# A fused cross-attention and mixture-of-experts kernel: slot numbers, products that read nothing and last sums moved, and the first chunk's queries projected in two halves

## The chip, the cores and the metric

The kernel runs on one core of a Trainium2 chip. A core has TensorE (PE, matmuls and transposes), VectorE (DVE), ScalarE (ACT), GpSimd (POOL) and SyncE (SP, which here only issues transfers). The metric is the device time of one execution in microseconds; lower is better. The kernel before was timed three times, and one more execution was profiled.

## The reference, cut to what matters

```python
x = x + tanh(g_xattn[0]) * xattn(layernorm(x), ctx)      # 32 sequences of 64 rows, 256 wide
# xattn: q, k_new, v_new = x @ wq.T, x @ wk.T, x @ wv.T
#        k, v = concat(cache, new);  softmax(q @ k.T / 16) @ v @ wo.T
x = x + tanh(g_ffn[0]) * ffn(layernorm(x))
# ffn: router = xf @ gate_w.T; softmax; top 2 of 8 experts
#      expert: (silu(xf @ fc1.T) * (xf @ fc2.T)) @ proj.T, 176 wide, weighted by the router
#      shared: the same with 704, times sigmoid(xf @ shared_gate_w.T)
```

All 2048 rows pass through both parts. The cache of keys and of values is the context, 64 rows for each sequence.

## The kernel before, in words

The program is written out by hand: for each engine there is one list of instructions, and semaphores tie the lists together. An engine takes its list strictly in order, so an instruction that waits holds up all that stand behind it on its engine.

A float32 operand is kept as two parts, "hi" (rounded to fp32r) and "lo" (the rest). A product is then a chain of three matmuls: hi*hi, hi*lo, lo*hi. For nearly every result in PSUM (the eight banks `B[0]` to `B[7]`) ACT copies it into a hi tile and DVE subtracts that from the bank into a lo tile; the next chain on PE waits for both. In the names of tiles `ew`, `sw`, `xt` and `sh` are large tiles that hold queries, keys, values, normalised rows and weights at different times.

The attention goes in four chunks `c` = 0 to 3 of 512 rows, each in four tiles `j` of 128 rows. While chunk `c` is attended, chunk `c+1` is normalised (`first_norm`, transposes on PE) and projected (`project`: `i` = 0, 1 the queries, 2, 3 the keys), and chunk `c-1` is normalised a second time and routed. For a tile: `scores` (PE), `row_max` (DVE), `exps` (ACT), `values` (PE), `v_hi` (ACT), `v_lo` (DVE), `probs_t` (PE), `probs_hi` (ACT), `probs_lo` (DVE), `attend` (PE), `residual` (DVE: reciprocal, scaled sum, statistics). `attend` waits in its second matmul for `v_lo` and in its third for `probs_lo`.

The router: `two_best(c)` and `counts(c)` on DVE find the two experts of each row and count them, `route(c)` on PE (two small matmuls) adds up the counts, `slots(c)` on DVE (seven small steps, each of which waits for the one before) makes of them a slot number for each row and expert, and `scatter(c, i)` on POOL writes the rows to these slots in DRAM with indirect transfers. The loops over `c` handle `slots(c-2)`, so slots of chunk 0 and 1 are made in loops 2 and 3.

Start: SP loads x of chunk 0 in two halves, then the four attention weights in three pieces, the context of chunk 0 (into `CR`), and x of chunk 1. ACT loads the gates, the constants (with the identity that transposes need) and the router's weights. `cached_hi(0)` (ACT) and `cached_lo(0)` (POOL, four subtractions) bring the context in as keys; behind `cached_lo(0)` in POOL's list stands `rstd1(1)`, four small steps, for which ACT's `first_apply(1)` waits. Behind the first half of `first_apply(1)` in ACT's list stands the copy of the product of the value and output weights (WVO), and `values(0, 0)` waits for it. SP loads the next context (`load_ctx(1)`) when `cached_lo(0)` is done, and behind it the router's constants and x of chunk 2. `warm(n)` on PE makes n transposes of the identity whose result nobody reads.

After the attention, the shared network runs over three chunks (`fc`, `s_silu`, `s_mult`, `s_hi`, `s_lo`, `pj`), then 39 expert tiles, then the shared network over the last chunk. During this last part the results of the experts are loaded back: `combine(n)`, n = 0 to 7, adds two tiles of them, the even n and n = 7 on DVE, 1, 3, 5 and 6 on POOL, and `s_last(t)` (DVE) adds the shared result to the last four tiles of rows. The order of the last chunk on DVE:

```python
for t in range(TPC):
    s_last(t)
combine(7)
```

The output goes out by chunks and tiles. SP stores, in this order: chunks 0 and 1, the half of chunk 2 that `combine(6)` makes, and two tiles of chunk 3. ACT stores the two other tiles of chunk 3 and then the half of chunk 2 that `combine(7)` makes.

## Time and profile before

| What | Value |
|---|---|
| Time, median of 3 runs | 294.89 us (294.42 to 295.42) |
| Time of the profiled execution | 294.28 us |
| Its span in the profile | 292.5 us |
| PE busy | 272.9 us (93%) |
| PEld (weight loads) busy | 245.7 us (84%) |
| DVE busy | 213.9 us (73%) |
| ACT busy | 170.7 us (58%) |
| POOL busy | 136.1 us (47%) |
| Chain that ended last, by engine | PE 57%, DVE 23%, issue 7%, ACT 6%, DMA 3%, POOL 1% |

The span runs from the first to the last instruction of the profile; the time of the same execution is 1.8 us longer. Busy shares are averages over all stages. The chain is followed back from the last instruction, at each step to what released it.

### The profile page before, as it was taken

How to read it: one execution, taken by the hardware profiler on the slowest of the kernel's cores; microseconds unless marked ns; L12 is line 12 of the kernel's file. 1: busy time of each engine (PE TensorE's matmuls, PEld its weight loads, DVE VectorE, ACT ScalarE, POOL GpSimd, SP SyncE). 2: the span in 40 equal slices, each digit the busy share in tenths (PEclk: the TensorE clock that was granted, in tenths of full speed). 3: DMA queues.
4: the chain of work that ended last, by engine and by line, in shares of the span. 5: the costliest groups of instructions: out<-in, count | busy, mean ns of one | idle time of the engine just before them, and what ended most of it. 6: DMA issues, size and time to landing. Idle time of an engine off the chain costs nothing.

```text
span 292.5 us, 5859 instructions
## 1 busy us (share of the span) xinstructions
PE 272.9 (93%) x1777; PEld 245.7 (84%) x1777; DVE 213.9 (73%) x694; ACT 170.7 (58%) x401; POOL 136.1 (47%) x161
## 2 busy tenths in 40 slices
PE   3998899999899899999999999899999999999992
PEld 3887789789778677888788888899999999998882
DVE  6867776979869759768776767868778777763285
ACT  2775678687566567473335446566666667654240
POOL 2420831441784427453450000068778778776141
PEclk9999999999999999999999999999999999999999
DMA  6470244221136112544425744368888888756796
GB/s 194 190 256 2 73 149 141 72 80 50 38 91 242 74 40 85 186 144 125 150 76 182 247 140 145 131 113 134 136 141 134 136 139 137 116 69 72 291 354 217
DMA packets 25022, 40.18 MB, mean 137 GB/s; under 512 B 2976, under 2 KB 18976, under 8 KB 24992
## 3 DMA queue, kind: packets, MB, share of 16 engines
q1 hardware_dynamic: 16272, 27.43, 29.1%
q0 software_dynamic: 7152, 9.57, 19.4%
q10 hardware_dynamic: 1568, 2.80, 2.7%
q8 instruction: 15, 0.25, 0.4%
q14 instruction: 15, 0.12, 0.2%
HBM read 22.68 MB, written 17.11 MB: 136 GB/s over the span
## 4 chain that ended last, share of the span: by engine, by line
PE 57%; DVE 23%; issue 7%; ACT 6%; DMA 3%; POOL 1%; SPq 0%; DVEq 0%; ACTq 0%; POOLq 0%
PE bank L437 43%; PE bank L702 8%; DVE ew_lo L1097 4%; DMA xn_all<-x_dram 3%; PE bank L801 3%; PE bank L755 3%; DVE work L1453 2%; ACT ew_hi L830 2%; DVE xt_lo L1097 2%; ACT sh_hi L830 2%; DVE neg_max L1145 2%; DVE sh_lo L1097 2%; DVE ln_stats L1108 1%; DVE work L1168 1%; ACT work L862 1%
## 5 line engine op out<-in xcount | busy, mean ns | idle before, releaser
L1650 POOL DMA_INDIRECT y_d<-work,dest_of_slot x39 | 60.5, 1552 | 56.2 <-DVE dest_of_slot L1504 54.7
L437 PE MATMUL bank<-ew_hi,xt_hi 128*128 (+2 forms) x172 | 53.9, 323 | 1.4 <-DVE xt_lo L1097 0.7
L437 PE MATMUL bank<-ew_lo,xt_hi 128*128 (+2 forms) x172 | 51.7, 301 | 0.0
L437 PE MATMUL bank<-ew_hi,xt_lo 128*128 (+1 forms) x133 | 40.5, 305 | 0.0
L1610 POOL DMA_INDIRECT xs_d<-xn_all,slot_of_pair x32 | 33.3, 1042 | 10.1 <-issue 7.3
L1097 DVE TENSOR_TENSOR xt_lo<-bank,xt_hi 128x256 fp32r<-128x256 f32 (+2 forms) x90 | 35.5, 397 | 3.2 <-ACT xt_hi L830 2.0
L437 PE MATMUL bank<-xt_hi,sw_hi 128*128 128x512 f32 x88 | 34.8, 395 | 0.2 <-DVE work L1453 0.2
L437 PE MATMUL bank<-xt_lo,sw_hi 128*128 128x512 f32 x88 | 34.5, 392 | 0.0
L437 PE MATMUL bank<-xt_hi,sw_lo 128*128 128x512 f32 x88 | 34.3, 390 | 0.0
L830 ACT ACTIVATE xt_hi<-bank 128x256 fp32r<-128x256 f32 (+1 forms) x90 | 32.7, 409 | 2.4 <-PE bank L801 1.1
L437 PEld LDWEIGHTS bank<-ew_hi,xt_hi 128*128 128x128 f32 (+1 forms) x172 | 32.4, 189 | 2.0 <-DVE xt_lo L1097 0.9
L437 PE MATMUL bank<-ew_hi 128*128 128x256 f32 (+1 forms) x100 | 30.8, 314 | 3.4 <-DVE ew_lo L1097 2.0
L437 PEld LDWEIGHTS bank<-ew_lo,xt_hi 128*128 128x128 f32 (+1 forms) x172 | 32.7, 190 | 0.1
L1097 DVE TENSOR_TENSOR ew_lo<-bank,ew_hi 128x512 fp32r<-128x512 f32 (+1 forms) x41 | 22.6, 580 | 13.2 <-ACT ew_hi L830 13.1
L830 ACT ACTIVATE sh_hi<-work 128x512 fp32r<-128x512 f32 (+1 forms) x24 | 15.2, 632 | 28.8 <-DVE work L1453 25.2
L437 PE MATMUL bank<-ew_hi,ew_lo 128*128 128x256 f32 (+1 forms) x100 | 30.4, 310 | 1.5 <-DVE ew_lo L1097 1.5
L437 PE MATMUL bank<-ew_lo,ew_hi 128*128 128x256 f32 (+1 forms) x100 | 29.7, 304 | 0.6 <-DVE ew_lo L1097 0.2
L702 PE MATMUL bank<-sw_hi,sh_hi 128*128 128x256 f32 x96 | 27.2, 289 | 0.3 <-DVE work L1468 0.2
L830 ACT ACTIVATE ew_hi<-bank 128x512 fp32r<-128x512 f32 (+1 forms) x45 | 21.6, 518 | 9.3 <-PE bank L437 8.2
L702 PE MATMUL bank<-sw_lo,sh_hi 128*128 128x256 f32 x96 | 26.6, 282 | 0.0
L437 PEld LDWEIGHTS bank<-ew_hi,xt_lo 128*128 128x128 f32 x133 | 25.1, 188 | 0.0
L1490 DVE TENSOR_TENSOR work<-work,bank 128x176 f32<-128x176 f32 x39 | 13.1, 337 | 16.0 <-ACT work L1025 16.0
(161 smaller groups left out, 678.8 us busy)
## 6 DMA issues: line engine op xcount, KB each, us to landing
work<-xs_d SPq DMA_DIRECT2D x39, 136.0 KB, 2.5
weight_stage<-ew_dram SPq DMA_DIRECT2D x10, 486.5 KB, 3.7
y_d<-work SPq DMA_DIRECT2D x6, 512.0 KB, 3.9
work<-ctx_t_dram SPq DMA_DIRECT2D x4, 512.0 KB, 3.3
ew_hi<-y_d SPq DMA_DIRECT2D x4, 512.0 KB, 8.1
ew_hi<-y_d ACTq DMA_DIRECT2D x4, 512.0 KB, 7.0
xn_all<-x_dram SPq DMA_DIRECT2D x3, 512.0 KB, 6.6
xs_d<-pad_row SPq DMA_DIRECT2D x9, 136.0 KB, 2.0
```

The source lines that it names most:

```text
L437: last = nc.tensor.matmul(dst, a, b, start=(n == 0), stop=(n == len(pairs) - 1))
L702: last = nc.tensor.matmul(B[4 + t][:, 0:D], h[:, t * P:(t + 1) * P], w, start=(j == 0 and n == 0), stop=(j == S_FULL and n == len(parts) - 1))
L755: last = nc.tensor.transpose(rows_bank(n)[:, k * P:(k + 1) * P], EX[:, w, k * P:(k + 1) * P], ident)
L801: last = nc.tensor.transpose(B[4 + v][:, i * P:(i + 1) * P], EH[:, v, i * P:(i + 1) * P], ident)
L830: return nc.scalar.activation(dst, src, ACT.Copy, scale=scale)
L862: nc.scalar.activation(XA[:, j, :], XNR[:, c * TPC + j, :], ACT.Identity, bias=nb1[:, j:j + 1], scale=rs1[:, j:j + 1]).then_inc(a_xn, 1)
L1097: return nc.vector.tensor_tensor(dst, src, hi.bitcast(F32), ALU.subtract)
L1145: last = nc.vector.tensor_reduce(nmx[r, j % 2:j % 2 + 1], own_keys(B[4 + j % 2], b), mybir.AxisListType.XY, ALU.max, negate=True)
L1453: nc.vector.tensor_tensor(SHF[0:rows, j % 2, :], STH[0:rows, j % 2, :], h2, ALU.mult).then_inc(v_h, 1)
L1490: nc.vector.tensor_tensor(EH[:, u % 2, 0:F_E], ETH[:, u % 2, :], B[2 + u % 2][:, F_E:2 * F_E], ALU.mult)
L1610: nc.gpsimd.indirect_dma_start(out=xs_d, out_offset=bass.IndirectOffsetOnAxis(ap=POS[:, i, n:n + 1], axis=0), in_=XN[:, n, :], in_offset=N ...
L1650: nc.gpsimd.indirect_dma_start(out=y2_d, out_offset=bass.IndirectOffsetOnAxis(ap=IX[:, n:n + 1], axis=0), in_=EY[:, n % 4, :], in_offset=None,
```

## The change

Eight things are moved or split.

1. SP loads x of chunk 1 ahead of the context of chunk 0; ACT loads the constants ahead of the gates.
2. PE starts with 13 products of the identity and not 10, has none between the two halves of `first_norm(0)`, and 3 and not 4 behind them.
3. The queries of chunk 0 are projected by `project_half(i, p)`, 256 rows at a time.
4. DVE makes `weight_lo(2)` and `weight_lo(3)` ahead of `project_lo(0, 0)`, and `ln1_stats(2)` two operations later.
5. `slots(c-2)` stands behind `aggregate(c, 0)` and no longer ahead of `v_lo(c, 1)`; `route(c-2)` stands behind `attend(c, 1)`, in bank 4 for chunks 0 and 1. `attend(c, 1)` no longer waits for the slots, `scores(3, 0)` does.
6. In loop 1, `scores` and `first_norm` alternate; in loop 2, `attend(2, 2)` and `residual(2, 2)` stand behind the projection of chunk 3's last keys.
7. POOL's `scatter` comes behind `rstd2` and one chunk's second half comes a loop later.
8. In the last shared chunk `fc` and `pj` are in another order, `combine(7)` stands ahead of `s_last`, and POOL's `combine(6)` waits until DVE has made the last `s_lo`.

```diff
+            load_x(1)
             sp.dma_start(CR, ctx_t[0]).then_inc(d_ct, 16)
-            load_x(1)
             load_ctx(1)
...
+            def project_half(i, p):
+
+                w, m = i // 2, i % 2
+                at = slice(p * 2 * P, (p + 1) * 2 * P)
+                waits = []
+                if i == 0:
+                    waits += [(0, a_xt, p + 1), (4, v_xt, p + 1)]
+                if m == 0 and p == 0:
+                    waits += [(0, wa_hi, w + 1), (2, wa_lo, w + 1)]
+                last = chain(B[(2, 3, 6, 7)[i]][:, at],
+                             [(WA[a][:, w, k, m * P:(m + 1) * P], XNT[0][b][:, k, at])
+                              for a, b in ((0, 0), (1, 0), (0, 1)) for k in range(KD)], waits)
...
-                if j == 1 and c > 1:
-                    waits = waits + [(0, v_pos, c - 1)]
...
-            warm(10)
+            warm(13)
             first_norm(0, 0)
-            warm(4)
             first_norm(0, 1)
-            warm(4)
-            for i in range(4):
+            warm(3)
+            for i in range(2):
+                project_half(i, 0)
+            for i in range(2):
+                project_half(i, 1)
+            for i in range(2, 4):
                 project(0, i)
...
                 attend(c, 1)
+                if c > 1:
+                    route(c - 2)
                 if c > 0:
                     router(c - 1)
...
-                attend(c, 2)
+                if c != LAST - 1:
+                    attend(c, 2)
                 values(c, 3)
                 probs_t(c, 3)
                 if c < LAST:
                     project(c + 1, 3)
-                else:
+                if c == LAST - 1:
+                    attend(c, 2)
+                if c == LAST:
...
             fc(LAST, 1)
+            pj(LAST, 0)
+            fc(LAST, 2)
+            fc(LAST, 3)
+            pj(LAST, 1)
+            fc(LAST, 4)
+            fc(LAST, 5)
             for j in range(2, S_BLK):
-                if j < S_FULL:
-                    pj(LAST, j - 2)
-                fc(LAST, j)
-            for j in range(S_FULL - 2, S_BLK):
                 pj(LAST, j)
...
                 residual(c, 0)
-                if c > 1:
-                    slots(c - 2)
                 v_lo(c, 1)
...
+                if c > 1:
+                    slots(c - 2)
                 v_lo(c, 2)
...
+            combine(7)
             for t in range(TPC):
                 s_last(t)
-            combine(7)
...
             for n in (1, 3, 5, 6):
+                if n == 6:
+                    pool.wait_ge(v_hl, 6 * N_CH)
                 combine(n)
```

The order of instructions is that of the lists. The first place is DVE's list at the start, before: the third and the sixth row subtract weights that lie in `weight_stage`, both operands in SBUF; the fifth is `project_lo(0, 0)`.

```order
L1097 TENSOR_TENSOR ew_lo<-weight_stage,ew_hi 128x512
L1108 BN_STATS ln1_stats<-xn2_all 128x6 x4
L1112 BN_AGGR ln1_mean_var<-ln1_stats 128x2 x4
L1135 SCALAR_TENSOR_TENSOR ew_lo<-bank2,ew_hi 128x512
L1097 TENSOR_TENSOR ew_lo<-weight_stage,ew_hi 128x512
L1317 SCALAR_TENSOR_TENSOR ew_lo<-weight_stage,tanh_gates,ew_hi 128x512
L1135 SCALAR_TENSOR_TENSOR ew_lo<-bank3,ew_hi 128x512
```

The same place now (lines are 34 higher):

```order
L1131 TENSOR_TENSOR ew_lo<-weight_stage,ew_hi 128x512
L1142 BN_STATS ln1_stats<-xn2_all 128x6 x4
L1146 BN_AGGR ln1_mean_var<-ln1_stats 128x2 x4
L1131 TENSOR_TENSOR ew_lo<-weight_stage,ew_hi 128x512
L1351 SCALAR_TENSOR_TENSOR ew_lo<-weight_stage,tanh_gates,ew_hi 128x512
L1169 SCALAR_TENSOR_TENSOR ew_lo<-bank2,ew_hi 128x512
L1169 SCALAR_TENSOR_TENSOR ew_lo<-bank3,ew_hi 128x512
```

The two subtractions of weights 2 and 3 have moved ahead of the one that reads bank 2.

The second place is DVE's list in loop 3, between the statistics of `residual(3, 0)` and `row_max(3, 3)`, before. The seven rows from L1259 to L1264 are `slots(1)`; the next three are `v_lo(3, 1)`, `second_lo(2, 1)` and `probs_lo(3, 1)`.

```order
L1172 BN_STATS ln2_stats<-work 128x6
L1259 TENSOR_TENSOR work<-work,bank7 128x32
L1260 TENSOR_REDUCE work<-work 128x4
L1259 TENSOR_TENSOR work<-work,bank7 128x32
L1260 TENSOR_REDUCE work<-work 128x4
L1261 TENSOR_SCALAR payload<-work,tanh_gates 128x4x2
L1262 SCALAR_TENSOR_TENSOR slot_of_pair<-work 128x2x4
L1264 COPY work<-work 128x8
L1097 TENSOR_TENSOR ew_lo<-bank2,ew_hi 128x512
L1097 TENSOR_TENSOR xt_lo<-bank0,xt_hi 128x2x256
L1097 TENSOR_TENSOR ew_lo<-bank1,ew_hi 128x256
L1145 TENSOR_REDUCE neg_max<-bank5 64x1 x2
```

The same place now, up to the first two of the seven rows:

```order
L1206 BN_STATS ln2_stats<-work 128x6
L1131 TENSOR_TENSOR ew_lo<-bank2,ew_hi 128x512
L1131 TENSOR_TENSOR xt_lo<-bank0,xt_hi 128x2x256
L1131 TENSOR_TENSOR ew_lo<-bank1,ew_hi 128x256
L1179 TENSOR_REDUCE neg_max<-bank5 64x1 x2
L1202 SCALAR_TENSOR_TENSOR work<-bank7,softmax_scale,xn2_all 128x256
L1206 BN_STATS ln2_stats<-work 128x6
L1212 BN_AGGR ln2_mean_var<-ln2_stats 128x2 x2
L1293 TENSOR_TENSOR work<-work,bank4 128x32
L1294 TENSOR_REDUCE work<-work 128x4
```

The slots now follow `residual(3, 1)` and its aggregate, and read bank 4.

The third place is the end of DVE's list, before; the first and the last row are `combine(4)` and `combine(7)`, the second is the last `s_lo`.

```order
L1440 TENSOR_TENSOR xn2_all<-ew_hi 128x2x256
L1097 TENSOR_TENSOR sh_lo<-work,sh_hi 128x512
L1483 SCALAR_TENSOR_TENSOR xn2_all<-bank4,shared_gate,xn2_all 128x256
L1483 SCALAR_TENSOR_TENSOR xn2_all<-bank5,shared_gate,xn2_all 128x256
L1483 SCALAR_TENSOR_TENSOR xn2_all<-bank6,shared_gate,xn2_all 128x256
L1483 SCALAR_TENSOR_TENSOR xn2_all<-bank7,shared_gate,xn2_all 128x256
L1440 TENSOR_TENSOR xn2_all<-ew_hi 128x2x256
```

The same place now:

```order
L1477 TENSOR_TENSOR xn2_all<-ew_hi 128x2x256
L1131 TENSOR_TENSOR sh_lo<-work,sh_hi 128x512
L1477 TENSOR_TENSOR xn2_all<-ew_hi 128x2x256
L1520 SCALAR_TENSOR_TENSOR xn2_all<-bank4,shared_gate,xn2_all 128x256
L1520 SCALAR_TENSOR_TENSOR xn2_all<-bank5,shared_gate,xn2_all 128x256
L1520 SCALAR_TENSOR_TENSOR xn2_all<-bank6,shared_gate,xn2_all 128x256
L1520 SCALAR_TENSOR_TENSOR xn2_all<-bank7,shared_gate,xn2_all 128x256
```

`combine(7)` has moved ahead of the four last sums.

## Rows read from the trace of the kernel before

**Rows 1.** Page, busy time, share of the span and instructions of each engine.

```profile
PE 272.9 (93%) x1777; PEld 245.7 (84%) x1777; DVE 213.9 (73%) x694; ACT 170.7 (58%) x401; POOL 136.1 (47%) x161
```

**Rows 2.** Waits of PE: us in total, times, longest.

```profile
PE bank L437 <- DVE ew_lo L1097: 3.7, 7, 1.5
```

**Rows 3.** Timeline of the start: start, us, engine, line, tiles, [idle before <-releaser].

```profile
10.33 1.06 ACT L830 ACTIVATE ew_hi<-work 128x1024 fp32r<-128x1024 f32 x1
11.47 2.83 POOL L1596 TENSOR_TENSOR ew_lo<-work,ew_hi 128x256 fp32r<-128x256 f32 x4 [4.48 <-ACT ew_hi L830]
11.67 1.41 DVE L1108 BATCH_NORM_STATS2 ln_stats<-xn_all 128x6 f32<-128x256 f32 x4 [0.57 <-DMA xn_all<-x_dram]
...
13.99 0.86 DVE L1097 TENSOR_TENSOR ew_lo<-weight_stage,ew_hi 128x512 fp32r<-128x512 f32 x1
...
14.25 0.65 POOL L1565 TENSOR_TENSOR ln_bias<-ln_mean_var,consts_sb 128x4 f32<-128x4 f32 x1
...
16.97 1.09 ACT L862 ACTIVATE work<-xn_all,ln_bias,ln_rstd 128x256 f32<-128x256 f32 x2 [0.67 <-POOL ln_bias L1570]
...
18.57 0.69 DVE L1097 TENSOR_TENSOR ew_lo<-bank,ew_hi 128x512 fp32r<-128x512 f32 x1 [1.27 <-ACT ew_hi L830]
...
21.69 0.87 ACT L830 ACTIVATE ew_hi<-bank 128x512 fp32r<-128x512 f32 x2
...
21.86 1.41 DVE L1108 BATCH_NORM_STATS2 ln_stats<-xn_all 128x6 f32<-128x256 f32 x4 [1.48 <-DMA xn_all<-x_dram]
...
23.71 1.02 DVE L1097 TENSOR_TENSOR ew_lo<-bank,ew_hi 128x512 fp32r<-128x512 f32 x2
```

**Rows 4.** Timeline of POOL in loop 0, the same small step one chunk later.

```profile
34.13 0.20 POOL L1565 TENSOR_TENSOR ln_bias<-ln_mean_var,consts_sb 128x4 f32<-128x4 f32 x1
```

**Rows 5.** Timeline of DVE and PE around the slots in loop 2.

```profile
74.22 0.17 DVE L1259 TENSOR_TENSOR work<-work,bank 128x32 f32<-128x32 f32 x1
...
77.43 0.39 PE L437 MATMUL bank<-ew_hi,ew_lo 128*128 128x256 f32 x1 [0.55 <-DVE ew_lo L1097]
```

**Rows 6.** Timeline of DVE at the end of loop 2.

```profile
87.09 0.69 DVE L1097 TENSOR_TENSOR sw_lo<-bank,sw_hi 128x512 fp32r<-128x512 f32 x1 [0.59 <-ACT sw_hi L830]
...
88.87 1.31 DVE L1145 TENSOR_REDUCE neg_max<-bank 64x1 f32<-64x128 f32 x4
```

**Rows 7.** Timeline of PE, ACT and DVE around the slots in loop 3.

```profile
95.24 0.30 PE L580 MATMUL bank<-work 128*128 128x32 f32 x2
...
95.60 0.30 PE L445 MATMUL bank<-consts_sb,xn_all 128*128 128x128 f32 x1
...
96.07 0.60 ACT L830 ACTIVATE ew_hi<-bank 128x512 fp32r<-128x512 f32 x1
...
96.19 0.17 DVE L1259 TENSOR_TENSOR work<-work,bank 128x32 f32<-128x32 f32 x1
...
97.66 0.68 DVE L1097 TENSOR_TENSOR ew_lo<-bank,ew_hi 128x512 fp32r<-128x512 f32 x1
...
99.32 0.38 PE L437 MATMUL bank<-ew_hi,ew_lo 128*128 128x256 f32 x1 [0.55 <-DVE ew_lo L1097]
```

**Rows 8.** Timeline of the end, engines and queues that issue transfers (SPq, ACTq).

```profile
285.10 1.27 POOL L1660 TENSOR_TENSOR xn_all<-ew_hi 128x512 f32<-128x512 f32 x1 [2.28 <-DMA ew_hi<-y_d]
285.19 1.72 DVE L1097 TENSOR_TENSOR sh_lo<-work,sh_hi 128x512 fp32r<-128x512 f32 x1
...
286.97 0.39 PE L702 MATMUL bank<-sw_hi,sh_lo 128*128 128x256 f32 x1 [1.25 <-DVE sh_lo L1097]
...
287.47 1.66 DVE L1483 SCALAR_TENSOR_TENSOR xn_all<-bank,shared_gate,xn_all 128x256 f32<-128x256 f32 x4 [0.56 <-PE bank L702]
...
289.76 0.39 ACTq L1090 DMA_DIRECT2D out_dram<-xn_all  x1
```

**Rows 9.** Stages of the end: us, busy time of the engines, PEclk, DMA share, GB/s.

```profile
286.20:288.20 2.00, 1.23 (x10) 1.24 (x10) 1.44 (x3) 0.00 (x0) 0.17 (x1) 1.00 1.05 365
...
288.70:291.60 2.90, 0.00 (x0) 0.00 (x0) 1.03 (x3) 0.00 (x0) 0.00 (x0) 1.00 0.80 271
```

61 lines of the change are left out of this document (41 added, 20 removed).

## The prediction

> **What bounds the kernel now.** I read the page first: PE is busy for 93% of the span, every other engine for at most 84% [rows 1]. No product of substance is taken away, so the change can only gain what PE stands still, and what lies behind its last matmul. I then read whom PE waits for: most often DVE's lo tiles, 3.7 us over 7 waits, 1.5 at the longest [rows 2]. I followed each such wait in the timeline. Four places matter. At the start a late x and a late WVO hold the chain [rows 3]; in loops 2 and 3 DVE makes slots while `attend` waits for lo tiles [rows 5, 7]; at the end DVE's last `s_lo` takes 1.72 us and PE waits 1.25 for it, and the stores follow [rows 8].
>
> **The loops (parts 5 to 7 of the change).** In loop 3 the copy `v_hi(3, 1)` ends at 96.07 + 0.60 = 96.67, so `v_lo(3, 1)` could start at 96.72. It starts at 97.66, because `slots(1)` runs from 96.19 until then, 1.47 us [rows 7]. What follows in DVE's list is `second_lo`, `probs_lo` and `row_max(3, 3)`, and PE's `attend(3, 1)` gets its third matmul off only when `probs_lo` is there, at 99.32. With the slots gone from this place all of it comes 97.66 - 96.72 = 0.94 us earlier. Loop 2 is alike: the slots begin at 74.22, the third matmul goes at 77.43 [rows 5], and I take 1.0.
>
> Where do the slots go? Behind the aggregate, where DVE would wait for the copy of `values(c, 2)`; before, it idles there for longer than the 1.47 us of slots. So they cost DVE nothing, but they bring `route` with them. Its matmuls hold PE for 95.60 - 95.24 = 0.36 us [rows 7], and they now stand between `attend(c, 1)` and `values(c, 2)`, on the path, where before they filled a wait. Loop 3 then keeps 0.94 - 0.36 = about 0.6.
>
> In loop 2 the 1.0 - 0.36 = 0.6 is carried on to `project(3, 3)`. Moving `attend(2, 2)` behind it lets PE work while DVE makes the last keys' lo tile, so `scores(3, 0)` starts over a microsecond earlier. But `residual(2, 2)` moves too, from a place where DVE was idle to one on DVE's path. Between the end of `project_lo(3, 3)`, 87.09 + 0.69 = 87.78, and `row_max(3, 0)` at 88.87 stand now one residual and the aggregate, 1.09 us [rows 6]. One more residual with its reciprocal, some 1.0 us, eats what the earlier `project_lo` brought. The row maxima, and with them the exponentials, win perhaps 0.2. So the two loops give 0.6 + 0.2 = 0.8 us. Bounds: 0.3, if the `residual` costs its full price and loop 3's projection takes over; 1.6, if both 0.94 and 1.0 less one 0.36 survive. The alternation in loop 1 I take at nothing: `probs_t(1, 0)` waits for ACT's exponentials, which are behind ACT's own list. Without that cover it would gain about 0.4. POOL's scatters are transfers nobody in the loops waits for.
>
> **The start (parts 1 to 4).** Before, the context lands in time for `cached_hi(0)` at 10.33 and x of chunk 1 lands 1.3 us later, at 11.67 [rows 3]. The two have the same size and the queue is one, so swapping them makes the context land at about 11.65. `cached_hi(0)` starts 1.3 us later, and everything on POOL behind it.
>
> There is more. In the before, DVE's subtraction of weight 2 at 13.99 took 0.86 us, and POOL's small step at 14.25 took 0.65, ending with it [rows 3]; the same step alone takes 0.20 [rows 4]. The two took turns. Both weight subtractions now stand ahead of `project_lo(0, 0)` and meet the four large POOL steps, 2.83 / 4 = 0.71 each; each time POOL waits for a DVE instruction, about 0.6 us. The small steps behind, no longer stretched, give 0.45 + 0.5 back. The Trainium skill says the same (SBUF — State Buffer, section "Who interferes with whom"): a DVE instruction with two SBUF inputs and a GpSimd one that reads SBUF exclude each other, each for its whole instruction. The trace agrees, by the 0.65 against 0.20.
>
> Sum for POOL: it starts at 11.47 + 1.33 = 12.8, its large steps end at 12.8 + 2.83 + 1.1 = 16.7, and the small ones at 0.2 + 0.2 + 1.0 + 0.2 and their gaps, 1.75, end at 18.45. Before, ACT's `first_apply(1)` could start at 16.97 [rows 3]; now 18.45, 1.5 us later. The WVO copy, its lo tile (18.57 before) and `values(0, 0)` follow 1.5 later.
>
> What does this cost? The chain was cut anyway: the two copies that begin with `v_hi(0, 0)` on ACT end at 21.69 + 0.87 = 22.56, the first of them near 22.3, but DVE stood before x of chunk 2 until 21.86, made its statistics, and only reached `v_lo(0, 0)` at 23.71 [rows 3]. These statistics are moved two operations on, so 23.71 - 22.3 = 1.4 us are won there and 1.5 lost: I take +0.1, a loss. The statistics, 1.41 and an aggregate, then fall into the wait for the next copy, which they overrun by about 0.3; the `project_lo(1, 0)` moved ahead of `residual(0, 0)` gives that back. The halves of the queries and the warm products bring PE's first projection forward by some 0.8 us, but behind it DVE's lo tiles, now behind two weights, come no earlier: nothing. Bounds: -0.9, if POOL and DVE do not get in each other's way (1.33 less 0.95 of unstretched steps is 0.4, against 1.4 won); +1.0, if they do so twice as much.
>
> **The end (part 8).** POOL's `combine(6)` started at 285.10, DVE's last `s_lo` at 285.19; POOL ended at 286.37, and DVE 0.54 later, at 286.91 [rows 8]. Without POOL the `s_lo` takes the 0.69 of its size (DVE at 18.57) [rows 3] and ends at 285.88, 1.03 earlier, and PE with it. The new order of `fc` and `pj` changes nothing at that place: the last `s_hi` waits for the third-last `pj` as before. Then DVE makes `combine(7)` (0.63, the time between 289.13, when the last sums end, and the store at 289.76) and the four sums in 1.66: 285.88 + 0.63 + 1.66 = 288.2, against 289.76 before.
>
> But the stores. POOL's `combine(6)` now starts at 286.5 and ends at 287.8, and three stores of SP stand behind it. So 256 KB that went out before 288.2 in the shadow now go last. From 287.9 on, 0.92 MB (two halves of chunk 2, three tiles) must go; the best rate of the end is 365 GB/s [rows 9], 2.5 us, and the first byte flows 0.7 after the issue. That ends at 287.9 + 0.7 + 2.5 = 291.1; before, the data ended near 291.5 (271 GB/s over the 2.9 us from 288.7) [rows 9]. With the mixed rate it is 291.3. I take -0.25. Bounds: 0, and -1.0 if the bytes don't bind: the last issue at 288.8 with the 2.7 us that stood between the last issue (289.76) and the end of the span (292.5) gives 291.5.
>
> The Trainium skill (DMA: Bandwidth & Descriptors, "Anatomy of one DMA") puts one transfer, fitted on GpSimd's own path, at 2.0 us plus its bytes at 436 GB/s. By that the last tile, issued at 288.8, would be down at 291.1, and the end would gain about 0.7. Rows 9 show a lower rate for tiles of this kind, and I use that.
>
> **Sum.** +0.1 - 0.8 - 0.25, about -1.0. Against the profiled execution, 294.28: 293.3. That run was 0.6 faster than the median of 294.89, and I forecast the median: 293.9.
>
> **Rivals.**
> - *The start wins too* (14%). If weight 2 and 3 find POOL idle or between steps, the loss of 1.5 becomes 0.4 and the start gives 0.9: 293.0. For it: DVE could slip in at step ends. Against: four steps back to back leave no hole.
> - *The end wins in full* (12%). The store traffic doesn't bind, 1.0 instead of 0.25: 293.1. Against it: rows 9 at share 1.05.
> - *The slots don't pay* (20%). Something stands in their shadow: the residual in loop 2 and `route` on PE in loop 3 take it all. The time is 294.89 - 0.2 = 294.6. This is also the case in which the change does not do what it says. For it: PE is dense after each of the places.
> - *The start loses* (10%). The context behind x holds POOL, POOL holds `first_apply(1)`, and WVO is late. It decides as soon as WVO comes later than the 1.4 us of cover. If every POOL step meets DVE, or the context lands another microsecond later, 1.5 to 2 us stand open, against the gain of 1.0: 295.6. For it speaks the turn-taking of rows 3; against it, that only two DVE steps there read SBUF twice. By the rule that the Trainium skill states of the shared port (SBUF — State Buffer), any further such step would add its whole length.
>
> **How the numbers follow.** The forecast, start even, loops 0.8, stores binding, has 44%. Under 0.3% (0.88 us) nothing can be told from no change. Of the forecast's own spread, 293.3 to 294.5, some two thirds lie beyond that bound. Faster: 0.44 x 0.66 + 0.14 + 0.12 = 0.55; slower: 0.08 of the last rival; the rest, 0.37, is the same. The range takes the two rivals below down to 292.8 and reaches up to 295.0, within the last one.
>
> **What would show it.** Start: `cached_hi(0)` at about 11.7, POOL's first small step after 16 us, 0.2 long, and `values(0, 0)` over 1 us later than 19.3, but `v_lo(0, 0)` near 23.8. Loops: in loop 3 `v_lo(3, 1)` right behind ACT's copy, and between the start of loop 2 and the first `fc` about 0.8 us less. End: the last `s_lo` at 0.69, PE's last wait at 0.3, `combine(6)` behind it, and a DMA share near 1 until the end. I am wrong if the stall before `v_lo(0, 0)` moves by more than 0.5 either way, or if the stores finish with the last sum.

## The result, and the profile after

The changed kernel takes 296.06 us in the median of 20 executions (295.08 to 298.83), the kernel before 295.06 in the same session (294.25 to 296.75, 20 executions). The ratio is 1.0046, 95% interval 1.0025 to 1.0066: 0.46% slower, where 0.3% faster was forecast. Seven of the 20 executions took 297.34 us or more, the profiled one (298.83 us, span 297.0) among them; the other 13 lie between 295.08 and 296.38, and their median is 296.03, so the long ones don't make the median.

The page of after, busy time (against [rows 1]):

```profile
PE 275.7 (93%) x1787; PEld 248.1 (84%) x1787; DVE 212.4 (72%) x694; ACT 170.4 (57%) x401; POOL 136.7 (46%) x161
```

PE is busy 2.8 us longer with nearly the same products: some of its matmuls ran slower. The start, timeline of after (against [rows 3]):

```profile
12.29 1.06 ACT L861 ACTIVATE ew_hi<-work 128x1024 fp32r<-128x1024 f32 x1 [1.92 <-DMA work<-ctx_t_dram]
13.43 3.73 POOL L1638 TENSOR_TENSOR ew_lo<-work,ew_hi 128x256 fp32r<-128x256 f32 x4 [5.69 <-ACT ew_hi L861]
...
14.63 1.22 DVE L1351 SCALAR_TENSOR_TENSOR ew_lo<-weight_stage,tanh_gates,ew_hi 128x512 fp32r<-128x512 f32 x1
...
17.12 0.20 POOL L1607 TENSOR_TENSOR ln_bias<-ln_mean_var,consts_sb 128x4 f32<-128x4 f32 x1
...
21.22 0.39 PE L437 MATMUL bank<-ew_hi 128*128 128x256 f32 x1 [1.23 <-DVE ew_lo L1131]
...
24.22 1.02 DVE L1131 TENSOR_TENSOR ew_lo<-bank,ew_hi 128x512 fp32r<-128x512 f32 x2 [1.93 <-ACT ew_hi L861]
```

POOL's four large steps take 3.73 us instead of 2.83, DVE's weight 3 takes 1.22, the small step is back at 0.20: the turns are taken as foreseen. `v_lo(0, 0)` starts 24.22 - 23.71 = 0.51 later. `values(0, 0)` (the PE row) starts 21.22 - 19.32 = 1.90 later; in the trace of the kernel before its row is this one:

```profile
19.32 0.39 PE L437 MATMUL bank<-ew_hi 128*128 128x256 f32 x1 [0.30 <-DVE ew_lo L1097]
```

Loop 3, timeline of after (against [rows 7]). The rows are, in order: the last of POOL's four indirect issues, the last matmul of `values(3, 1)`, the end of `exps(3, 2)`, `v_hi(3, 1)`, the first matmul of `attend(3, 1)`, the third, one of a later product, and the first product of the expert tiles:

```profile
95.23 0.96 POOL L1652 DMA_INDIRECT xs_d<-xn_all,slot_of_pair  x1 [0.30 <-issue]
...
95.37 0.28 PE L437 MATMUL bank<-ew_hi,sw_lo 128*128 128x256 f32 x1
...
96.16 0.19 ACT L922 ACTIVATION_READ_ACCUMULATOR work<-bank,neg_max 64x1 f32 x1
...
97.18 0.60 ACT L861 ACTIVATE ew_hi<-bank 128x512 fp32r<-128x512 f32 x1 [0.84 <-remote]
...
98.60 0.39 PE L437 MATMUL bank<-ew_hi 128*128 128x256 f32 x1 [1.58 <-ACT ew_hi L861]
...
99.48 0.58 PE L437 MATMUL bank<-ew_hi,ew_lo 128*128 128x256 f32 x1 [0.38 <-DVE ew_lo L1131]
...
104.04 0.41 PE L437 MATMUL bank<-ew_hi,xt_lo 128*128 128x256 f32 x1
...
186.40 0.43 PE L437 MATMUL bank<-ew_hi,xt_hi 128*128 x1 [0.65 <-DVE xt_lo L1131]
```

`values(3, 1)` ends at 95.65 and ACT is free at 96.35, yet its copy starts at 97.18; the view names no engine that it waited for. PE then stands still for 1.58 us in one piece. Before, PE waited at this place too, but for half as long:

```profile
97.89 0.35 PE L437 MATMUL bank<-ew_hi 128*128 128x256 f32 x1 [0.73 <-DVE work L1264]
```

Stages of after: us, busy time of the engines, PEclk (granted clock), DMA share, GB/s:

```profile
95.50:99.40 3.90, 2.02 (x16) 1.60 (x14) 2.59 (x7) 2.19 (x7) 0.69 (x1) 1.00 0.21 79
99.40:106.20 6.80, 6.72 (x27) 5.72 (x28) 2.92 (x14) 1.93 (x6) 3.37 (x7) 0.50 0.17 61
106.20:111.70 5.50, 5.32 (x34) 4.45 (x35) 3.55 (x10) 2.65 (x8) 2.03 (x3) 1.00 0.21 76
```

Behind that stall the clock is at half (1.2 and not 2.4 GHz) for 6.80 us, and the matmuls in it take up to twice their step. From the third matmul of `attend(3, 1)` to the first of `attend(3, 2)` it takes 106.69 - 99.48 = 7.21 us; in e9 below, the same kernel at full clock, 102.85 - 98.41 = 4.44. So the fall costs 2.8 us in this execution.

The end, timeline of after (against [rows 8]); the third row is `combine(6)`:

```profile
287.85 0.36 PE L731 MATMUL bank<-sw_hi,sh_hi 128*128 128x256 f32 x1 [0.16 <-DVE sh_hi L1131]
...
288.45 0.69 DVE L1131 TENSOR_TENSOR sh_lo<-work,sh_hi 128x512 fp32r<-128x512 f32 x1
...
289.22 1.69 POOL L1702 TENSOR_TENSOR xn_all<-ew_hi 128x512 f32<-128x512 f32 x1 [3.06 <-DVE sh_lo L1131]
...
289.70 1.66 DVE L1520 SCALAR_TENSOR_TENSOR xn_all<-bank,shared_gate,xn_all 128x256 f32<-128x256 f32 x4
...
291.36 1.04 SPq L425 DMA_DIRECT2D out_dram<-xn_all  x2
291.39 0.45 ACTq L1124 DMA_DIRECT2D out_dram<-xn_all  x1
```

The last `s_lo` takes 0.69 and PE's long wait is gone, as predicted. But the last sum ends at 291.36 and the span at 297.0, 5.7 us later; before, 289.13 and 292.5, 3.4. The half clock of loop 3 moves the whole end of this run, but not this last stretch, and the stretch is 2.3 us longer.

### The profile page after: what moved, and what is told of

Its sections match the earlier page's. It is cut to its first block, busy times and chain, and to the rows that moved or that the text cites. A ratio compares the mean times of both kernels' runs of the same rounds, so it can differ in the third digit from the quotient of the medians.

```text
span 297.0 us, 5880 instructions
## 1 busy us (share of the span) xinstructions
PE 275.7 (93%) x1787; PEld 248.1 (84%) x1787; DVE 212.4 (72%) x694; ACT 170.4 (57%) x401; POOL 136.7 (46%) x161
## 3 DMA queue, kind: packets, MB, share of 16 engines
HBM read 22.68 MB, written 17.11 MB: 134 GB/s over the span
## 4 chain that ended last, share of the span: by engine, by line
PE 61%; DVE 15%; issue 9%; ACT 9%; POOL 2%; DMA 1%; another core or an unknown queue 0%; DVEq 0%; ACTq 0%; POOLq 0%
PE bank L437 45%; PE bank L731 9%; DVE ew_lo L1131 4%; ACT ew_hi L861 3%; PE bank L830 3%; PE bank L784 3%; DVE neg_max L1179 2%; ACT work L922 2%; DVE xt_lo L1131 2%; DVE ln_stats L1142 1%; DMA xn_all<-x_dram 1%; POOL ew_lo L1638 1%; ACT work L893 1%; ACT xn_all L898 1%; ACT sh_hi L861 1%
## 5 line engine op out<-in xcount | busy, mean ns | idle before, releaser
L1652 POOL DMA_INDIRECT xs_d<-xn_all,slot_of_pair x32 | 33.4, 1043 | 10.2 <-issue 7.3
L437 PE MATMUL bank<-ew_hi 128*128 128x256 f32 (+1 forms) x104 | 31.4, 311 | 4.1 <-DVE ew_lo L1131 2.1
L437 PEld LDWEIGHTS bank<-ew_hi 128*128 128x128 f32 x104 | 19.3, 189 | 6.9 <-DVE ew_lo L1131 2.8
```

The source lines that it names most:

```text
L437: last = nc.tensor.matmul(dst, a, b, start=(n == 0), stop=(n == len(pairs) - 1))
L1652: nc.gpsimd.indirect_dma_start(out=xs_d, out_offset=bass.IndirectOffsetOnAxis(ap=POS[:, i, n:n + 1], axis=0), in_=XN[:, n, :], in_offset=N ...
```

## The experiments

All medians in us. The runs were made in five sessions on four chips: e1 to e4, e5 to e8, e9 to e12, e13 to e16, e17 and e18. The kernel before ran in each beside them, with medians of 295.13, 295.27, 295.25, 294.99 and 295.04. Times of one session compare best.

"Low" counts the executions whose mean granted clock, over the whole span, is 0.993 or less. It is a rough sign of a fall of the clock that costs time, because the clock also falls where PE has nothing left to do: in 18 of the 20 profiles it is at half at the very end, behind PE's last product. In e13 that is the only fall. Stage of e13:

```profile
291.20:296.90 5.70, 0.00 (x0) 0.00 (x0) 0.00 (x0) 0.00 (x0) 0.00 (x0) 0.50 0.18 62
```

PE's last product there ends at 289.43, and yet the mean clock is 0.990. In the kernel before PE is idle for 4.1 us at the end, which can lower the mean to 0.993 and no further; 51 of its 135 executions are at 0.992 or less and so have a fall elsewhere, if their ends are like the profiled one's. In the change and in e3 PE is idle for 6.4 us there. Of the 15 low executions of the change, eight (0.992 or 0.993) took 295.6 to 296.4 us, like its five others; only the seven long ones stand apart.

| Kernel | Median | Ratio to before, 95% | Low |
|---|---|---|---|
| the change | 296.06 | 1.0046 [1.0025, 1.0066] | 15 of 20, 7 of them long |
| e1 parts 1 to 4 | 295.14 | 1.0004 [0.9976, 1.0032] | 2 of 12 |
| e2 parts 5 to 7 | 295.75 | 1.0025 [0.9994, 1.0055] | 4 of 12 |
| e3 part 8 | 296.57 | 1.0051 [1.002, 1.0082] | 6 of 12 |
| e4 part 8, no wait | 295.04 | 0.9995 [0.9966, 1.0024] | 4 of 12 |
| e5 part 5 | 299.86 | 1.016 [1.0121, 1.0199] | 6 of 6 |
| e6 parts 6, 7 | 296.58 | 1.0036 [1.0014, 1.0058] | 7 of 12 |
| e7 parts 5 to 7, route first | 292.89 | 0.9928 [0.9909, 0.9948] | 0 of 12 |
| e8 change, no wait | 293.8 | 0.9958 [0.9941, 0.9976] | 1 of 12 |
| e9 the change again | 295.2 | 1.0003 [0.9982, 1.0023] | 1 of 12 |
| e10 change, no wait, route first | 292.89 | 0.9926 [0.9904, 0.9948] | 0 of 6 |
| e11 e2 with late scatters | 293.17 | 0.9933 [0.9911, 0.9956] | 0 of 6 |
| e12 e2 with filler | 294.41 | 0.9974 [0.9955, 0.9992] | 1 of 12 |
| e13 before, POOL late | 298.38 | 1.0109 [1.0044, 1.0174] | 4 of 4, see above |
| e14 change, combine(6) on DVE | 292.7 | 0.9926 [0.9899, 0.9952] | 0 of 11 |
| e15 e10, late scatters | 292.83 | 0.9933 [0.9908, 0.9959] | 1 of 12 |
| e16 e10 without parts 1 to 4 | 293.46 | 0.9942 [0.9915, 0.9969] | 0 of 12 |
| e17 e10, combine(6) on DVE | 293.39 | 0.9957 [0.9926, 0.9989] | 6 of 12 |
| e18 e15, combine(6) on DVE | 292.86 | 0.9926 [0.99, 0.9951] | 0 of 9 |

### The change in pieces: e1 to e4

Each is the kernel before with some parts of the change and no other edit. e1 has parts 1 to 4.

```diff
+            load_x(1)
             sp.dma_start(CR, ctx_t[0]).then_inc(d_ct, 16)
```

> The kernel before with parts 1 to 4 of the change alone. Theory A (three causes: the start costs about 0.5, the end about 1.1, and the loops, which should gain about 1, lose it again because PE's granted clock falls to its half level behind a stall in loop 3): +0.5 us against the kernel before, cached_hi(0) near 11.7 to 12.3, POOL's four large steps 1.0 us apart instead of 0.71, and values(0, 0) 1.5 to 1.9 us later than 19.32, v_lo(0, 0) 0.4 to 0.6 later than 23.71; no fall of the granted clock to 0.5 between 20 and 280 us. Rival B (the start is even, as predicted; the later x in the trace of after was chance): within 0.2 us of before.

Measured: 295.14, no difference. Rival B holds: the start is even. Its trace has `values(0, 0)` at 20.85, 1.53 late, and `v_lo(0, 0)` at 23.85, 0.14 late, as the prediction said.

e2 has parts 5 to 7.

```diff
                 attend(c, 1)
+                if c > 1:
+                    route(c - 2)
```

> The kernel before with parts 5 to 7 alone (slots and route, the alternation, attend(2, 2), scatters). Theory A: in runs with a clock of 0.998 or more it is 0.7 to 1.0 us faster than before (about 294.0 against 294.9), and some runs, with a clock of 0.985 to 0.993, are 2 to 3 us longer than that, because PE stands for over 1 us ahead of attend(3, 1) in one piece; the median then lands near level. Rival C (the fall of the clock comes from the start's shift or is a one-off of that trace): all runs 0.7 to 1.0 faster, none with a clock below 0.996.

Measured: 295.75, not told apart from before. Its profile repeats the picture of after: `v_hi(3, 1)` 0.73 late, PE's stall 1.50, and from 100.7 to 104.1 the half clock:

```profile
96.92 0.60 ACT L841 ACTIVATE ew_hi<-bank 128x512 fp32r<-128x512 f32 x1 [0.73 <-PE bank L437]
...
98.34 0.39 PE L437 MATMUL bank<-ew_hi 128*128 128x256 f32 x1 [1.50 <-ACT ew_hi L841]
```

Its four low executions took 296.78 to 297.64. The eight others, 295.21 in the mean, aren't faster than those of before at such clocks (294.67, 20 of the 35 of that session), so the falls of the clock are not all. A late signal alone would explain it: in this trace the third matmul of `attend(3, 1)` starts 99.23 - 89.06 = 10.17 us after `row_max(3, 0)`, in e9, with the signal on time, 98.41 - 88.94 = 9.47. By that a late signal costs 0.7 us, as much as the loops gain. How many of the eight had it isn't known.

e3 has part 8, e4 the same without these lines:

```diff
-                if n == 6:
-                    pool.wait_ge(v_hl, 6 * N_CH)
```

> The kernel before with part 8 alone. Theory A: +1.1 us: PE's last wait falls from 1.25 to 0.2 or 0.3 us, but from PE's last matmul to the end of the span it takes 6.3 us and not 4.1, since combine(6) waits for the last s_lo and four of SP's and ACT's stores are issued behind it. Rival D (the late end in the trace of after was a matter of the clock or of chance; the forecast of the end was right): -0.25 us, last data within 3 us of PE's last matmul.

> The kernel before with part 8, but without the wait ahead of combine(6): only the order of fc and pj, and combine(7) ahead of the last sums. Theory A (the wait is what costs the end): PE's last wait is 1 us or more again, stores issued early again, and the time is within 0.3 of before, 1 us below the run with the wait. Rival E (the order of combine(7) and of fc and pj costs the time): as long as the run with the wait, +0.8 to +1.1 us.

Measured: 296.57 and 295.04. Two lines, 1.5 us. The other moves of the end give nothing that can be told. Theory A is right on the end, and the prediction's -0.25 is wrong.

### Loops: e5 to e7, and the change without the wait: e8

e5 has part 5 alone, e6 has parts 6 and 7.

```diff
-                if c > 1:
-                    slots(c - 2)
                 v_lo(c, 1)
```

> The kernel before with part 5 alone: slots and route moved. What is known: parts 5 to 7 together came out 0.6 us slower in the median and 0.5 slower among the runs with a clock of 0.994 or more, and in two traces with them ACT's v_hi(3, 1) starts 0.84 and 0.73 us after ACT is free, though PE's last matmul of values(3, 1) ended 1.5 us earlier. Theory F (the move of route and slots is what makes the signal late and PE's stall ahead of attend(3, 1) long): v_hi(3, 1) late by 0.7 or more here too, PE idle for 1.5 to 1.8 us in one piece ahead of attend(3, 1), +0.3 to +0.8 us in the median. Rival G (the lateness belongs to part 6, since it also came with attend(2, 2) moved): v_hi(3, 1) right behind exps(3, 2), and 1.0 us faster than before.

Measured: 299.86, 4.6 us slower, and neither theory had the reason. Timeline of e5: the last of POOL's scatters, its `rstd2(2, 1)`, ACT's `second_apply` and PE's second norm:

```profile
93.91 0.96 POOL L1612 DMA_INDIRECT xs_d<-xn_all,slot_of_pair  x1 [0.30 <-issue]
94.89 0.21 POOL L1567 TENSOR_TENSOR ln_bias<-ln_mean_var,consts_sb 128x2 f32<-128x2 f32 x1
...
96.35 1.09 ACT L869 ACTIVATE xn_all<-work,ln_bias,ln_rstd 128x256 f32<-128x256 f32 x2 [4.54 <-POOL ln_bias L1572]
...
97.49 0.66 PE L445 MATMUL bank<-consts_sb,xn_all 128*128 128x128 f32 x4 [2.54 <-ACT xn_all L869]
```

The slots come later, so the scatters behind them do, 1.27 us apart, and POOL's small steps for the next norm stand behind them. PE waits 2.54 us for that norm, and from 98.4 us on the clock is at half for 10.2 us:

```profile
98.40:108.60 10.20, 8.91 (x35) 7.69 (x36) 6.32 (x22) 3.77 (x12) 1.56 (x3) 0.50 0.08 30
```

So the loss is the stall and the fall together. All six executions are low. The times go with the clock: 298.1 and 299.0 at 0.992, 299.5 to 301.5 at 0.983 and less. Part 7 moves the scatters out of the way. Parts 5 and 7 are one edit.

> The kernel before with parts 6 and 7 alone: alternation, attend(2, 2) and residual(2, 2), scatters. Theory F: v_hi(3, 1) on time, slots still ahead of v_lo(3, 1); time between -0.3 and +0.2 of before. Rival G: v_hi(3, 1) late, and +0.3 to +0.8.

Measured: 296.58, slower. `v_hi(3, 1)` is on time, so rival G is out, but the size is wrong as well. In its trace `row_max(3, 0)` starts at 89.57 and not at 88.87 [rows 6], 0.12 of it already there at `row_max(2, 0)`: both residuals stand ahead of it. Later the slots still stand ahead of `v_lo(3, 1)`, and `attend(3, 1)` waits 1.27 us for them and then 0.55 for `probs_lo`. Behind that the clock falls here too, with no late signal:

```profile
100.40:103.80 3.40, 3.34 (x11) 2.68 (x12) 1.65 (x7) 1.28 (x5) 0.68 (x3) 0.51 0.22 80
```

e7 is e2 with route in PE's stall.

```diff
-                attend(c, 1)
                 if c > 1:
                     route(c - 2)
+                attend(c, 1)
```

> Parts 5 to 7, with route(c - 2) ahead of attend(c, 1) and not behind it; the slots stay where part 5 puts them. Theory F: route now runs in PE's stall, so it costs nothing and cuts the idle time in two; 0.36 us better than parts 5 to 7 in any case, and up to 1.3 us better (293.9 to 294.5, faster than before) if the late signal comes from PE's running from values(3, 1) to scores(3, 3) without any other work behind it. Rival H (the order on PE does not matter to the signal; it is held up by something else): v_hi(3, 1) late by 0.7 as before, gain of 0.3 over parts 5 to 7, time 295.2 to 295.5.

Measured: 292.89, 2.4 us faster than before, better than the best case of the expectation. Timeline of e7, the two products of route and the first and third matmul of `attend(3, 1)`:

```profile
96.15 0.31 PE L582 MATMUL bank<-work 128*128 128x32 f32 x2
96.29 0.39 PE L583 MATMUL bank<-work 128*128 128x32 f32 x2
97.08 0.39 PE L437 MATMUL bank<-ew_hi 128*128 128x256 f32 x1 [0.41 <-ACT ew_hi L841]
...
98.21 0.39 PE L437 MATMUL bank<-ew_hi,ew_lo 128*128 128x256 f32 x1 [0.54 <-DVE ew_lo L1108]
```

The third matmul goes at 98.21 against 99.32 before [rows 7]. No execution was low. Of the 2.4 us, 1.4 stand in the two profiles (spans of 291.1 and 292.5); part of the rest is that 13 of the 29 executions of the kernel before were low in that session: their median is 295.97, that of the others 294.81.

> The changed kernel without the wait ahead of combine(6), all else as changed. If the causes add up, it is 1.4 us faster than the changed kernel (the difference between the runs of part 8 with the wait, 296.57, and without it, 295.04), so near 295.1 to 295.4. Rival (the wait costs only where the store queue is in the state of before; in the changed kernel the start and the loops set the time): no more than 0.5 us faster than the changed kernel's 296.06.

e8 is the change with the two lines of e4 taken out. Measured: 293.8, faster than before and than foreseen. The expectation compared with the change in another session; against e9, the same kernel with the wait, the two lines are worth the 1.4 it foresaw.

e8 and e7 ran in one session. Both have parts 5 to 7; e8 has parts 1 to 4 and part 8 without the wait beside them, which changed nothing in e1 and e4. What is left between them is the place of route, worth 293.8 - 292.89 = 0.9 us. By the same token e8 should be level with e2, and it is 2.0 us faster. So parts 5 to 7 gave no gain in e2's session and 1.5 us in e8's. The profile of e2 has the late signal and that of e8 has not; that this is the reason isn't shown.

### The same again, and the clock: e9 to e12

e9 has no edit.

> The changed kernel once more, on the same chip as the three others, with a second profile. If ACT's late v_hi(3, 1) and the fall of the granted clock behind it are part of this program, both are in this profile too, near 97 and 99 to 106 us, and the time is about 1.0 above before. If they were chance, this profile has v_hi(3, 1) right behind exps(3, 2) and a time near 295.3.

Measured: 295.2, level with before, one low execution of 12. Its profile has `v_hi(3, 1)` on time, and the clock stays at full until the end. Timeline of e9:

```profile
95.89 0.19 ACT L922 ACTIVATION_READ_ACCUMULATOR work<-bank,neg_max 64x1 f32 x1
...
96.10 0.60 ACT L861 ACTIVATE ew_hi<-bank 128x512 fp32r<-128x512 f32 x1
...
97.51 0.38 PE L437 MATMUL bank<-ew_hi 128*128 128x256 f32 x1 [0.78 <-ACT ew_hi L861]
...
98.41 0.39 PE L437 MATMUL bank<-ew_hi,ew_lo 128*128 128x256 f32 x1 [0.39 <-DVE ew_lo L1131]
...
182.55 0.43 PE L437 MATMUL bank<-ew_hi,xt_hi 128*128 x1 [0.59 <-DVE xt_lo L1131]
...
285.24 1.69 POOL L1702 TENSOR_TENSOR xn_all<-ew_hi 128x512 f32<-128x512 f32 x1 [3.17 <-DVE sh_lo L1131]
```

The fifth row is the first product of the expert tiles. In the trace of the kernel before it is this one, in the same view:

```profile
183.08 0.43 PE L437 MATMUL bank<-ew_hi,xt_hi 128*128 x1 [0.72 <-DVE xt_lo L1097]
```

So the late signal and the fall in loop 3 are not fixed in the program's text: the same kernel has long executions in one session, 7 of 20, and none in another.

That e9 is level with the kernel before is partly the other's doing: 8 of the 23 executions of the kernel before were low beside it. Above 0.993 it has a median of 294.66 and e9 of 295.16. The change is 0.5 us slower there, as between the two profiles (spans of 293.0 and 292.5).

> The changed kernel without the wait ahead of combine(6) and with route(c - 2) ahead of attend(c, 1). If the two repairs add up: 293.8 (without the wait) less 0.4 to 1.0 for route, so 292.8 to 293.4, which would be 2 us or 0.7% faster than before. If parts 1 to 4 (the start) cost 0.5, it stays 0.5 behind parts 5 to 7 with route ahead alone (292.89).

e10 joins the edits of e7 and e8 on the whole change. Measured: 292.89, as expected: 1.4 for the wait and 0.9 for route, within one session with e9. It is no worse than e7, so parts 1 to 4 cost nothing here.

e11 is e2 with no indirect transfer issued in loop 3.

```diff
-                if c == LAST:
-                    scatter(c - 3, 1)
...
             rstd2(LAST, 1)
-            scatter(LAST - 2, 1)
+            scatter(0, 1)
+            scatter(1, 0)
+            scatter(1, 1)
```

> Parts 5 to 7 on the kernel before, with the second half of chunk 0's scatter and the first of chunk 1's behind loop 3, so that POOL issues no indirect transfer in loop 3. In the traces so far late signals of PE (ACT's v_hi(3, 1) 0.7 to 0.8 late, and smaller ones) all end 1.7 to 1.9 us after the start of the last of four indirect issues. Theory I (POOL's indirect issues hold up PE's signals): v_hi(3, 1) right behind exps(3, 2), PE's idle time ahead of attend(3, 1) 0.9 us and not 1.7, no fall of the clock, time 0.6 to 1.4 below parts 5 to 7 (294.4 to 295.2). Rival: v_hi(3, 1) late all the same.

e12 is e2 with ten products that nobody reads.

```diff
+                if c == LAST:
+                    for _ in range(10):
+                        nc.tensor.transpose(B[3][:, 0:P], ident, ident)
                 attend(c, 1)
```

> Parts 5 to 7 on the kernel before, with 10 transposes of the identity into the free bank 3 ahead of attend(3, 1): about 1.1 us of work without use in PE's stall. Theory J (the fall of the granted clock is what makes parts 5 to 7 slower, and PE's idle piece brings it): no run with a clock under 0.993, and the median 0.5 or more below parts 5 to 7 (295.75), although nothing is computed sooner. Rival (the clock follows something else, or the time is lost in the waits themselves): the same clocks as parts 5 to 7, and the same time or up to 0.3 longer.

Measured: e11 293.17, below its range, `v_hi(3, 1)` on time and no low execution. e12 294.41, 0.8 faster than before and 1.3 us below e2, with one low execution. Neither shows what it was made for. Both expectations take e2's 295.75 as their base, and that belongs to another session; against e8 (293.8, and 293.8 is also what e9 of their own session gives without the 1.4 of its wait), whose loops are those of e2, e11 is 0.6 faster and e12 0.6 slower. So that the ten products made the kernel faster isn't shown. Both profiles had the signal on time, so neither shows the late signal cured. The counts don't decide either: e11, e15 and e18, which issue nothing indirect in loop 3, have one low execution of 27, but e7, e10, e14 and e16, which do, have none of 41.

### What the end waits for: e13 and e14

```diff
+            pool.wait_ge(v_z, 14)
+            pool.wait_ge(a_xn2, 4 * N_CH)
+            nc.gpsimd.tensor_tensor(nb2[:, 0:2], nb2[:, 0:2], C[:, C_HALF:C_HALF + 2], ALU.mult)
```

> The kernel before with one more small instruction at the end of POOL's list, which waits for DVE's last sum; no transfer and nothing else is moved. In 11 of 13 traces so far the span ends 6.12 us after POOL's last instruction, combine(6), whatever the stores do. Theory K (POOL needs about 6 us behind its last instruction before the program can end, and this, not the stores, makes part 8 slow): the small instruction ends near 289.4, so the span ends near 295.5, 3.0 us later than before. Rival L (the end waits for the stores that combine(6) releases): they are as early as before, so no difference, within 0.2 us.

```diff
-            for n in (1, 3, 5, 6):
-                if n == 6:
-                    pool.wait_ge(v_hl, 6 * N_CH)
+            for n in (1, 3, 5):
                 combine(n)
...
+            combine(6)
             combine(7)
```

> The changed kernel with combine(6) on DVE, behind the last s_lo and ahead of combine(7), and no longer on POOL; its store is as late as in the change, the other stores 0.6 us later still. Theory K: POOL has its last instruction 3 us or more earlier, the end is now set by the stores: 0.5 to 1.2 us faster than the changed kernel. Rival L: no faster, or 0.3 to 0.6 slower.

Measured: 298.38, 3.4 slower than before, and 292.7, 2.3 faster than before, with which e9 is level. e13 has four executions only, 296.71 to 299.94. Timeline of e13, whose span is 296.9: POOL's added step and the last store.

```profile
290.23 0.57 POOL L1666 TENSOR_TENSOR ln_bias<-ln_bias,consts_sb 128x2 f32<-128x2 f32 x1 [2.85 <-DVE xn_all L1483]
290.79 0.39 ACTq L1090 DMA_DIRECT2D out_dram<-xn_all  x1
```

290.23 + 0.57 + 6.10 = 296.9. Timeline of e14, whose span is 291.5: POOL's last step and the last stores.

```profile
281.65 1.29 POOL L1703 TENSOR_TENSOR xn_all<-ew_hi 128x512 f32<-128x512 f32 x1 [0.75 <-DMA ew_hi<-y_d]
...
287.80 1.13 SPq L425 DMA_DIRECT2D out_dram<-xn_all  x2
288.58 0.47 ACTq L1124 DMA_DIRECT2D out_dram<-xn_all  x1
```

Theory K holds from both sides: making POOL late with the stores as they were costs 3.4 where it says 3.0, and making POOL early with its store as late as in the change gives more than it says. The traces place both behind PE's last product: from there to the end of the span it takes 4.1 us before, 7.5 in e13, 6.4 in e9 and 4.2 in e14. Rival L is out, since in e13 the last byte is down 4.3 us ahead of the end.

### Together: e15 to e18

e15 is e10 with the edit of e11, e16 is e10 on the start of before, e17 and e18 are e10 and e15 with the edit of e14.

> The changed kernel without the wait ahead of combine(6), with route ahead of attend(c, 1), and with no indirect transfer issued in loop 3. Route ahead gave 292.89 and the late scatter alone 293.17, from parts 5 to 7 at 295.75. Both cure the same stall, so together I expect little more: 292.4 to 292.9. If they cure two different things, 291.5.

> Parts 5 to 8 without the wait ahead of combine(6) and with route ahead of attend(c, 1), on the start of the kernel before (parts 1 to 4 undone). Against the same with parts 1 to 4, 292.89: if the start costs 0.3 to 0.5, this is at 292.4 to 292.6; if it is even, as the prediction had it, 292.9.

> The change with the two repairs that the runs point to: route(c - 2) ahead of attend(c, 1), and combine(6) on DVE, so that POOL is done 6 us and more ahead of the end. Each alone gave 292.9 and 292.7. The first is worth about 0.9 in loop 3 and the end is then set by the stores: with combine(6) on DVE PE's last wait is also gone, which the version with it on POOL and no wait still has (1.07 us). So 292.7 less 0.6 to 1.0: 291.7 to 292.1. If the end has nothing left to give behind POOL's 6 us, 292.6.

> The same, and no indirect transfer issued in loop 3 (the second half of chunk 0's scatter behind it). With route ahead of attend(c, 1) the late scatter gave nothing that could be told (292.83 against 292.89), so within 0.2 of the run beside it; if late signals of PE in loop 3 still cost something in part of the runs, its spread is smaller and its median 0.2 to 0.4 lower.

Measured: 292.83, 293.46, 293.39 and 292.86. e15 adds nothing to e10, so late scatters give nothing on top of route ahead. e16 is not better than e10 or e15, so the start isn't a loss; it is 0.6 slower, within the intervals. e17 missed its expectation by over a microsecond: six of its executions were low. Its profile, the fastest execution of the twelve at 292.31, is the third with the late signal, and it has no fall: with route in the stall PE waits 1.13 us in one piece. ACT's rows in e17:

```profile
95.20 0.19 ACT L922 ACTIVATION_READ_ACCUMULATOR work<-bank,neg_max 64x1 f32 x1
96.14 0.60 ACT L861 ACTIVATE ew_hi<-bank 128x512 fp32r<-128x512 f32 x1 [0.75 <-PE bank L437]
```

The six others have a median of 292.57. e18, without indirect issues in loop 3, has none low and 292.86, the same as e15, which has `combine(6)` on POOL. So moving it to DVE adds nothing that can be told on top of route ahead and no wait; the stores then set the end. e7, e10, e14, e15 and e18 stand within 0.2 us of each other, 0.7% below the kernel before; which of them is best the runs don't tell.

## Why the prediction was wrong

**The step that failed is in the part on the end:** "The stores [...] I take -0.25", with bounds of 0 and -1.0. It asked only when the data is down. In the undisturbed trace of the change, e9, PE's last matmul ends 288.41 - 286.66 = 1.75 earlier than before, as foreseen, but the span ends at 293.0 where the one before ends at 292.5. `combine(6)` ends at 285.24 + 1.69 = 286.93, and 6.1 us later the span ends. Before it is 285.10 + 1.27 = 286.37 [rows 8] and 292.5: the same 6.1. In 15 of the 20 traces the span ends 6.10 to 6.12 us after POOL's last instruction, whatever that is. In the other five (e1, e12, e14, e17, e18) POOL is 6.8 to 9.0 ahead, and the span ends 0.8 us after the last byte stored. The prediction moved the last instruction of POOL by 1.4 us (286.5 for 285.10) and costed the three stores behind it, not the ending of POOL itself. In the trace of before both limits nearly coincide: its last byte is down 0.9 us ahead of the end, so by an estimate from these five the stores alone would have ended it 0.15 earlier. That hid the one behind the other. The stores by themselves came out as forecast or better: in e9 the last byte is down at 290.62, before at 291.56, 0.94 earlier, of which e9 had 0.53 in hand. (The 0.7 us from an issue to its first byte stands in no row; for the last store of before the trace has 0.9, from 289.76 to 290.66.) The table sets the traces side by side (starts, and the ends of PE's last product and of the span):

| us | before | e9 | e7 | after |
|---|---|---|---|---|
| `row_max(1, 0)` | 43.16 | 43.28 | 43.28 | 43.57 |
| `row_max(2, 0)` | 65.81 | 65.94 | 65.94 | 66.23 |
| `row_max(3, 0)` | 88.87 | 88.94 | 88.52 | 89.22 |
| third matmul of `attend(3, 1)` | 99.32 | 98.41 | 98.21 | 99.48 |
| first expert product | 183.08 | 182.55 | 181.94 | 186.40 |
| end of PE's last product | 288.41 | 286.66 | 287.03 | 290.65 |
| end of the span | 292.5 | 293.0 | 291.1 | 297.0 |

At the first expert product e9 is 0.53 ahead of before, and at the end of the span 0.5 behind. The end costs 1.0, where 0.25 of gain stood in the sum. The wait alone is worth 1.5 in e3 against e4 and 1.4 in e9 against e8.

**No rival had this.** "The end wins in full" was the only one on the end, and no rival priced a fall of TensorE's clock. The one on the losing side, "the start loses", got 10%, and it is the wrong place. Its 295.6 lies near the measured 296.06 by luck alone.

**The start, +0.1: right.** The mechanism came as told (`cached_hi(0)` late, turns taken, `values(0, 0)` 1.90 late, cover used up); e1 measures 1.0004, e16 against e10 shows no loss, and e9 is 0.12 behind at `row_max(1, 0)`. In after `v_lo(0, 0)` was 0.51 late and not 0.1, in a run whose context came 0.6 later than reckoned. One trace says little here, since the start is where executions differ: `row_max(1, 0)` starts at 43.16 to 44.45 in the eleven profiles with the old start and at 42.98 to 44.20 in the nine with the new one (medians 43.39 and 43.20), while the time from there to `row_max(2, 0)` is 22.64 to 22.68 in all twenty. The rival "the start wins too", at 0.9, has no support.

**The loops, -0.8: right in an undisturbed run.** From `row_max(2, 0)` to `row_max(3, 0)` e9 gains 0.06, less than the 0.2 foreseen. From there to the third matmul of `attend(3, 1)` it takes 9.47 us for 10.45, a gain of 0.98 where 0.94 was read; e8 has 9.46. Then route takes its share, as predicted, and 0.6 is left of loop 3 at the first expert product: 0.7 for the loops. The bound of 0.3 to 1.6 holds. That route is on the path was right, and it was worth more than the step said, because it is on the path in loop 2 as well: with it ahead of `attend(c, 1)`, e7 gains 0.4 more than e9 in loop 2 and 0.2 more in loop 3. The prediction had route on the path there too, but reckoned that the residual ate nearly all that was left; with route out of the way `row_max(3, 0)` came 0.4 earlier all the same. "POOL's scatters are transfers nobody in the loops waits for" was wrong as a general sentence (e5), and did no harm only since part 7 is in the change.

**What the prediction did not see at all:** in part of the executions of the change the loops' gain turns into a loss. PE's signals to ACT come late, ACT's copy starts 0.7 to 0.8 late, PE's stall ahead of `attend(3, 1)` grows from 0.78 in e9 to 1.50 and 1.58 us, and behind it the granted clock is at half for 3.4 and 6.8 us. The stall is what the fall follows, not the late signal as such: e6 has a fall with the signal on time and waits of 1.27 and 0.55, e17 has the late signal, a wait of 1.13 and no fall.

The falls don't explain the result, though. If the seven long executions of 20 are those with a fall, the median without them is still 296.03, 0.8 us above e9. So of the 0.46% (1.0 us), the end is the part that every run shows, 1.0 to 1.5 us. In e9 the loops' 0.7 stands against it; in the session of the result nothing of that gain is seen, and why stays open. A late signal without a fall would cost about as much (0.7, see e2), but only one execution of that session was profiled.

What stays open: what holds up PE's signals. In all three profiles `v_hi(3, 1)` starts 1.9 us after the start of the last of POOL's four indirect issues (97.18 against 95.23 in after), but eight profiles with such issues in the same place have the signal on time, and the counts of low executions don't side with either view. Where the low executions of the kernel before have their fall is open too: no profile of it caught one. e14's has one at another place, from 18.8 to 22.2 us, and with a mean clock of 0.994 it isn't even counted as low. And what POOL does in the 6.1 us behind its last instruction no view tells.

## What to carry to other kernels

- Ask of every engine when its last instruction ends, not only when the last data is down: here POOL needs 6.1 us behind its last one, so the last step on POOL belongs on another engine or early in the end.
- A small job on PE costs its time on the path and little or nothing in a stall. Route ahead of `attend(c, 1)` was 0.9 us better than behind it. Look for the stall first, then put the job there.
- When a job's producer is moved later, go through every list behind its consumers (slots, scatters, then the next norm's small steps), and test such parts together.
- Take the base of a comparison from the same session. e2 and e8 have the same loops and stand 2.0 us apart; what e12 seemed to win over e2 is gone against e8. And look at where the clock is low before counting low executions: eight of the change's fifteen were no slower than the rest.
